# Bias products moved ahead of the sums they open, the selection tree's copies and placements dealt out anew, and the tail ordered by blocks of times

## What is computed

```python
w = weights[subjects]; b = bias[subjects]
h = einsum('bct,bcd->bdt', x, w) + b[:, :, None]
gate = silu((h @ fp8(gate_w)) * gate_scale)      # 256 -> 768
up = (h @ fp8(up_w)) * up_scale                  # 256 -> 768
out = x + ((gate * up) @ fp8(down_w)) * down_scale   # 768 -> 256
```

## Time and profile before

| | us |
|---|---|
| median of 3 runs (lowest, highest) | 52.18 (52.13, 52.43) |
| the profiled execution's own time | 52.42 |
| its span, first to last instruction | 50.6 |
| TensorE (PE) busy | 44.4 (88%) |
| VectorE (DVE) busy | 39.4 (78%) |
| ScalarE (ACT) busy | 25.9 (51%) |
| GpSimd (POOL) busy | 8.5 (17%) |

### The profile page before, as it was taken

One profiled execution on the slowest core, in us unless ns is written; L12 is line 12 of the kernel. 1 busy time (PEld: TensorE's weight loads), 2 busy tenths in 40 slices (PEclk: granted clock), 3 DMA queues, 4 the chain that ended last, 5 costly groups with the idle time before them and its releaser, 6 DMA issues.

```text
span 50.6 us, 667 instructions
## 1 busy us (share of the span) xinstructions
PE 44.4 (88%) x204; PEld 33.2 (66%) x204; DVE 39.4 (78%) x75; ACT 25.9 (51%) x43; POOL 8.5 (17%) x17
## 2 busy tenths in 40 slices
PE   2998999399999999969999999999999999999000
PEld 1331297398878787558878787887878788968000
DVE  2748898996757989999998769999684955896910
ACT  0951408945369095392807809572366394971000
POOL 3039605559600000000000000000000000360000
PEclk9999999999999999999999999999999999999999
DMA  0799999999900000000000000000000000019083
GB/s 0 165 349 366 356 371 402 418 419 414 379 23 0 0 0 0 0 0 13 0 0 0 0 6 0 0 0 0 0 0 0 0 0 0 0 49 371 2 299 115
DMA packets 2579, 5.71 MB, mean 113 GB/s; under 512 B 400, under 2 KB 912, under 8 KB 2576
## 3 DMA queue, kind: packets, MB, share of 16 engines
q1 hardware_dynamic: 2288, 5.53, 29.3%
q10 hardware_dynamic: 288, 0.15, 1.0%
HBM read 4.63 MB, written 1.05 MB: 112 GB/s over the span
## 4 chain that ended last, share of the span: by engine, by line
PE 56%; DVE 22%; DMA 5%; ACT 4%; issue 3%; POOL 3%; DVEq 1%; POOLq 0%
PE gu L538 33%; PE acc L546 19%; DMA subj_i<-in_subjects_dram 5%; DVE fuse L432 4%; PE acc L514 4%; DVE tree_sb L393 3%; POOL cond_bd L323 3%; DVE gu L393 3%; DVE f_lo L440 3%; DVE w_q L355 3%; ACT f_hi L269 2%; DVE res L445 2%; ACT silu L262 1%; DVE cond_bd L400 1%; PE acc L520 1%
## 5 line engine op out<-in xcount | busy, mean ns | idle before, releaser
L538 PE MATMUL gu<-h_hi,w_q 128*128 128x512 f32 (+1 forms) x52 | 15.1, 378 | 0.4 <-DVE w_q L355 0.4
L538 PE MATMUL gu<-h_lo,w_q 128*128 128x512 f32 (+1 forms) x52 | 15.0, 376 | 0.0
L269 ACT CAST f_hi<-fuse 128x512 fp32r<-128x512 f32 (+1 forms) x13 | 7.6, 588 | 12.7 <-DVE fuse L432 12.7
L538 PEld LDWEIGHTS gu<-h_hi,w_q 128*128 128x128 f32 x52 | 9.4, 187 | 2.8 <-issue 0.8
L440 DVE TENSOR_TENSOR f_lo<-fuse,f_hi 128x512 fp32r<-128x512 f32 (+1 forms) x13 | 8.4, 648 | 3.6 <-ACT f_hi L269 3.5
L538 PEld LDWEIGHTS gu<-h_lo,w_q 128*128 128x128 f32 x52 | 9.4, 187 | 2.0
L432 DVE SCALAR_TENSOR_TENSOR fuse<-gu,const_in,silu 128x512 f32<-128x512 f32 (+1 forms) x13 | 9.1, 705 | 1.4 <-issue 0.7
L262 ACT ACTIVATE silu<-gu,const_in 128x512 f32<-128x512 f32 (+1 forms) x13 | 8.4, 646 | 0.9 <-PE gu L538 0.8
L546 PE MATMUL acc<-f_hi,w_q 128*128 128x512 f32 (+1 forms) x26 | 7.9, 380 | 0.0
L546 PE MATMUL acc<-f_lo,w_q 128*128 128x512 f32 (+1 forms) x26 | 7.9, 382 | 0.0
L337 POOL TENSOR_TENSOR res<-y_sc,x_tok 128x512 f32<-128x512 f32 x1 | 1.3, 1297 | 30.4 <-ACT y_sc L283 30.4
(11 more groups left out here) (36 smaller groups left out, 24.6 us busy)
## 6 DMA issues: line engine op xcount, KB each, us to landing
w_in<-in_weights_dram SPq DMA_DIRECT2D x5, 384.0 KB, 6.4
x_sb<-in_x_dram SPq DMA_DIRECT2D x2, 512.0 KB, 4.3
x_tok<-in_x_by_time_dram SPq DMA_DIRECT2D x1, 1024.0 KB, 9.2
out_dram<-res SPq DMA_DIRECT2D x3, 256.0 KB, 2.1
w_in<-in_weights_dram SPq DMA_DIRECT2D x1, 256.0 KB, 3.8
const_in<-in_consts_dram SPq DMA_DIRECT2D x1, 151.0 KB, 2.3
w_in<-in_weights_dram SPq DMA_DIRECT2D x1, 128.0 KB, 5.4
out_dram<-res ACTq DMA_DIRECT2D x1, 128.0 KB, 2.0
```

The costliest lines, as they stand in the source:

```text
L269: nc.scalar.copy(f_hi[:, s % SLOTS, cols], fuse[:, s % SLOTS, cols]).then_inc(f_hi_made, 1)
L538: last = nc.tensor.matmul(gu[:, (s + q) % 2, part, cols], w_q[:, i, col:col + P], h[:, n, k, cols], start=(v == 0 and k == 0), stop=(v == ...
```

## The change

Five parts. (1) The bias products open the sums in `acc` (`bias_of(n)`, two products before `condition(n)`) and the last conditioning product of a bank signals `h_made`; the 12 products on zeros become 9, none tied to the tree; masks move from an `acc` bank to a `gu` bank. (2) ScalarE alone copies the even matrices for both halves, the tree of half 0 is in one bank. (3) Half 1 is placed by ScalarE (j = 0, 1, behind `high_of_h(0, 0)`) and GpSimd (j = 2, 3). (4) On VectorE tile 0 is rounded before `power(1)`; so ScalarE's `big(1)` goes behind `high_of_h(1, 1)`, GpSimd rounds tile 1 in two pieces (gate, up), TensorE waits for each piece apart, `big(4)` and `power(3)` move. (5) In the tail TensorE runs block 0 of step 9 ahead of step 11's gate and up and its block 1 behind; steps 10 and 11 also by blocks; `finish(0, 0)` runs inside step 10 on VectorE, `y_sc` on ScalarE goes behind the last `round_of`; half 1 is finished and stored whole by blocks, in four stores, not five.

```diff
-    WARM = (8, 2, 1, 1)
+    WARM = 9
...
-        tree = [t.rearrange("p (q g d) -> p q g d", g=GH, d=D) for t in (gu_flat[:, 512 + 256:1024 + 256], tree_sb)]
-        bits_ps = acc[:, 3, 0:BITS * G].bitcast(I32).rearrange("p (k g) -> p k g", g=G)
+        tree = [t.rearrange("p (q g d) -> p q g d", g=GH, d=D) for t in (gu_flat[:, 512:1024], tree_sb)]
+        bits_ps = gu[:, 1, 1, 0:BITS * G].bitcast(I32).rearrange("p (k g) -> p k g", g=G)
...
-        POOL_PIECES = ((1, 0, GU),)
+        POOL_PIECES = ((1, 0, GU // 2), (1, GU // 2, GU))
+
+        ACT_BLOCKS = ((0, 1), (0, 1))
+        POOL_BLOCKS = ((), (2, 3))
+        DVE_BLOCKS = ((2, 3), ())
...
             sp.wait_ge(res_dve, 1)
             store(0, 0, TOK)
-            sp.wait_ge(res_pool, 1)
-            store(1, 0, TOK)
             sp.wait_ge(res_dve, 2)
             store(0, TOK, 2 * TOK)
-            sp.wait_ge(res_dve, 4)
-            store(1, TOK + TOK // 2, 2 * TOK)
-            sp.wait_ge(stored, 16 * 5)
+            sp.wait_ge(res_dve, 3)
+            store(1, TOK, 2 * TOK)
+            sp.wait_ge(stored, 16 * 4)
...
             act.wait_ge(const_ld, 16)
-            nc.scalar.copy(tree[0][:, 2:PAIRS], cond_rep[:, 2:PAIRS, 0].unsqueeze(2).to_broadcast([P, 2, GH, D])
-                           ).then_inc(tree_even[0], 1)
-            nc.scalar.copy(tree[1], cond_rep[:, :, 0].unsqueeze(2).to_broadcast([P, PAIRS, GH, D])
-                           ).then_inc(tree_even[1], 1)
+            for n in range(HALVES):
+                nc.scalar.copy(tree[n], cond_rep[:, :, 0].unsqueeze(2).to_broadcast([P, PAIRS, GH, D])
+                               ).then_inc(tree_even[n], 1)
 
...
-                groups = slice(n * GH, (n + 1) * GH)
...
             place(0)
             high_of_h(0, 0)
+            place(1)
             big(0)
             high_of_h(0, 1)
-            big(1)
             high_of_h(1, 0)
             high_of_h(1, 1)
+            big(1)
...
                 silu_of(s)
                 if s == 0:
                     big(2)
+                elif s == 3:
+                    big(4)
                 round_of(s)
-                if s in (1, 2):
-                    big(s + 2)
+                if s == 1:
+                    big(3)
                 elif s in (4, 5):
                     big(s + 1)
 
...
-            act.wait_ge(down_made, HALF_DONE[0] + 1)
-            nc.scalar.activation(y_sc[:], acc[:, 1], ACT.Copy, scale=down_col[:, 1:2]).then_inc(y_scaled, 1)
             for q in range(LAST):
                 silu_of(STEPS - 1, q, PIECES[q])
             for q in range(LAST):
                 round_of(STEPS - 1, q, PIECES[q])
 
-            act.wait_ge(res_dve, 3)
-            act.dma_start(out_rows[:, 1, TOK:TOK + TOK // 2], res[:, 1, 1, 0:TOK // 2]).then_inc(stored, 16)
+
+            act.wait_ge(y0_made, 2)
+            nc.scalar.activation(y_sc[:], acc[:, 1], ACT.Copy, scale=down_col[:, 1:2]).then_inc(y_scaled, 1)
+            act.wait_ge(res_pool, 1)
+            act.dma_start(out_rows[:, 1, 0:TOK], res[:, 1, 0]).then_inc(stored, 16)
...
-            for j in range(J):
-                rows = slice(j * C, (j + 1) * C)
-                nc.gpsimd.tensor_copy(cond_bd[rows, GH:G, j * D:(j + 1) * D], tree[1][rows, 0]
-                                      ).then_inc(cond_placed[1], 1)
+            for j in POOL_BLOCKS[1]:
+                nc.gpsimd.tensor_copy(*block_of(1, j)).then_inc(cond_placed[1], 1)
...
                     if k == 0:
-                        dve.wait_ge(tree_even[n], 2 - n)
+                        dve.wait_ge(tree_even[n], 1)
...
             dve.wait_ge(const_ld, 16)
-            nc.vector.tensor_copy(tree[0][:, 0:2], cond_rep[:, 0:2, 0].unsqueeze(2).to_broadcast([P, 2, GH, D])
-                                  ).then_inc(tree_even[0], 1)
             dve.wait_ge(bits_made, 2)
             select(0)
             dve.wait_ge(bd_zeroed, 1)
-            place(0)
+            dve.wait_ge(tree_level[0], BITS)
+            for j in DVE_BLOCKS[0]:
+                nc.vector.tensor_copy(*block_of(0, j)).then_inc(cond_placed[0], 1)
             select(1)
...
             power(0, 0, GU)
             rest_of_h(0, 0)
-            power(1)
             add_big(0)
             take_big(0)
+            power(1)
             rest_of_h(0, 1)
             rest_of_h(1, 0)
             rest_of_h(1, 1)
...
                     take_big(2)
+                    power(3)
...
+                elif s == STEPS - 2:
+                    dve.wait_ge(x_tok_ld, 16)
+                    dve.wait_ge(y0_made, 1)
+                    finish(0, 0)
                 rest_of(s)
...
                     take_big(1)
                 elif s == 1:
-                    power(3)
                     add_big(2)
...
-            dve.wait_ge(x_tok_ld, 16)
-            dve.wait_ge(down_made, HALF_DONE[0] + 1)
-            finish(0, 0)
...
-            dve.wait_ge(y_made, 1)
-            finish(1, 0)
-            dve.wait_ge(y_made, 2)
-            for cols in PIECES:
-                finish(1, 1, cols)
+            for b in range(TB):
+                dve.wait_ge(y1_made, b + 1)
+                finish(1, b)
...
-            pe.wait_ge(warm_set, 1)
-            keep_warm(WARM[0])
-            for k in range(BITS):
-                pe.wait_ge(tree_level[0], k + 1)
-                keep_warm(WARM[k + 1])
...
-            for n in range(HALVES):
+            def bias_of(n):
+
+                pe.wait_ge(ones_made, 1)
+                pe.wait_ge(bias_placed, n + 1)
+                for k in range(KC):
+                    nc.tensor.matmul(acc[:, KC * n + k], ones_r[:], bias_tok[:, n * TOK // D:(n + 1) * TOK // D],
+                                     start=True, stop=False, skip_group_check=True)
+
+            def condition(n):
                 pe.wait_ge(cond_placed[n], J)
...
-                    bank = acc[:, KC * n + k]
                     for g in range(GH):
-                        nc.tensor.matmul(bank[:, g * P:(g + 1) * P], x_sb[:, n * GH + g, k * P:(k + 1) * P],
-                                         cond_bd[:, n * GH + g], start=(g == 0), stop=False,
-                                         skip_group_check=True)
-                    if k == 0:
-                        pe.wait_ge(ones_made, 1)
-                        pe.wait_ge(bias_placed, n + 1)
-                    nc.tensor.matmul(bank, ones_r[:], bias_tok[:, n * TOK // D:(n + 1) * TOK // D],
-                                     start=False, stop=True, skip_group_check=True).then_inc(h_made, 1)
+                        last = nc.tensor.matmul(acc[:, KC * n + k, g * P:(g + 1) * P],
+                                                x_sb[:, n * GH + g, k * P:(k + 1) * P], cond_bd[:, n * GH + g],
+                                                start=False, stop=(g == GH - 1), skip_group_check=True)
+                    last.then_inc(h_made, 1)
+
+            pe.wait_ge(warm_set, 1)
+            keep_warm(WARM)
+            for n in range(HALVES):
+                bias_of(n)
+                condition(n)
...
-                wait_quant(pe, i, 0)
                 for v, part in GU_ORDER[s < 2]:
+                    if v == 0:
+                        wait_quant(pe, i, part * KC * P)
...
+            def down_times(s, b):
+
+                pe.wait_ge(f_lo_made, s + 1)
+                down_block(s, 0, b)
+                return down_block(s, 1, b)
...
-            down(STEPS - 1 - LAG)
+
+
+            s = STEPS - 1
+            for i in (IC - 2, IC - 1):
+                wait_quant(pe, i, GU)
+            down_times(s - 2, 0).then_inc(y0_made, 1)
             for q in range(LAST):
-                gate_up(STEPS - 1, q, PIECES[q])
-            down(STEPS - 2)
-
-            s = STEPS - 1
-            wait_quant(pe, STEP[s][0], GU)
-            for q in range(LAST - 1):
-                for v, part_made in enumerate((f_hi_made, f_lo_made)):
-                    pe.wait_ge(part_made, s + q + 1)
-                    for b in range(TB):
-                        down_block(s, v, b, PIECES[q])
-            pe.wait_ge(f_hi_made, STEPS + LAST - 1)
-            down_block(s, 0, 0, PIECES[LAST - 1])
-            pe.wait_ge(f_lo_made, STEPS + LAST - 1)
-            down_block(s, 1, 0, PIECES[LAST - 1]).then_inc(y_made, 1)
-            down_block(s, 0, 1, PIECES[LAST - 1])
-            down_block(s, 1, 1, PIECES[LAST - 1]).then_inc(y_made, 1)
+                gate_up(s, q, PIECES[q])
+            down_times(s - 2, 1).then_inc(y0_made, 1)
+            down_times(s - 1, 0)
+            pe.wait_ge(f_hi_made, s + 1)
+            down_block(s, 0, 0, PIECES[0])
+            pe.wait_ge(f_lo_made, s + 1)
+            down_block(s, 1, 0, PIECES[0])
+            pe.wait_ge(f_hi_made, s + 2)
+            down_block(s, 0, 0, PIECES[1])
+            down_times(s - 1, 1)
+            pe.wait_ge(f_lo_made, s + 2)
+            down_block(s, 1, 0, PIECES[1]).then_inc(y1_made, 1)
+            for v in range(2):
```

(35 more changed lines are left out.)

7 lines of the change are left out of this document (5 added, 2 removed).

## The result

| | before | after |
|---|---|---|
| median of 20 runs (lowest, highest), us | 52.46 (52.13, 52.62) | 52.05 (51.92, 52.48) |
| profiled execution, us | 52.42 | 51.97 |
| its span, us | 50.6 | 50.2 |

The ratio of after to before is 0.9953, 95% interval 0.9933 to 0.9973: half a per cent faster, where 3.4% was forecast. 1.8 us were expected and 0.4 came. The profile after shows an opening that went almost to the hundredth as worked out, and two places behind it where the gain is given back.

What follows compares the result with a forecast made beforehand. TensorE was taken to bound the kernel from 22.00 us on, with gains only ahead of that and in the tail. Last finish 1.56 to 2.06 sooner, less 0.1 for the store, taken as 1.8: 52.18 to 50.4 us, range 49.9 to 51.4.

Steps and rivals of the forecast that it cites:

- Tree of half 0: Opening: ScalarE's copy of all pairs lets VectorE's first masked copy start at 3.72, not 4.04; 0.32 us won.
- Bias first: Conditioning of half 0: bias products leave the end of each bank, so rounding of h starts at 7.19, 0.55 sooner.
- Half 1 on two engines: Placement of half 1 by ScalarE and GpSimd: condition(1) starts at 8.72, not 9.73; 1.01 us won.
- Tile 0 first: VectorE's rounding before the gate: tile 0 ready at 10.58, first gate product at 10.64 against 12.09; 1.45 us won.
- Tile 1 late: GpSimd rounds tile 1 from 12.47 to 15.5 or 15.7; step 2's up part waits 0.2 to 0.4 us.
- TensorE's speed: Rival on both halves' conditioning: TensorE stays at its lower speed, time 53.6 us; chance 0.05.
- Tile 2 for step 4: VectorE's rounded weights come at 20.20, so step 4 starts at 20.3 instead of 22.00; 1.7 us won.
- Tail: Last products, finishes and stores: last finish ends at 46.15 or 46.65 against 48.21; larger last store costs 0.1 us.
- ends some 0.5 before: In the tail, the path over ScalarE and GpSimd (y_sc, add, store) ends some 0.5 us before the last store.
- the wait of the first tail product for f_lo: In the tail, step 9's pair of block 0 waits for the rest of f; 0.2 or 0.7 us lost.
- The gap put down to "issue" on VectorE: Steps 4 to 10: a 0.73 us gap ahead of a fuse; if it stays, VectorE's line is only about 1.1 ahead.
- VectorE's line sets the end: Rival: slips at tile 2 or take_big(3), the gap and tail losses leave 1.0 to 1.2 won, 51.1 us; chance 0.18.

Runs made afterwards that it cites:

- run 9: Changed kernel with 2 products on zeros instead of 9; ratio to the kernel before 1.0195 from two of four executions, median of all four 53.71 us.
- Run 4: Changed kernel with GpSimd only copying tile 1's gate and up columns, their fp8 rounding left out; ratio to the kernel before 0.9883.
- run 5: Changed kernel with VectorE's power(1) ahead of add_big(0) and ScalarE's big(1) behind high_of_h(0, 1) again, so GpSimd rounds tile 1 earlier; ratio to before 0.9874.
- run 10: Changed kernel with half 1 placed by GpSimd alone again (four copies); ratio to the kernel before 1.0143.
- run 1: Changed kernel with all tail edits (part 5) undone; ratio to before 0.9899 without its two longest executions, median of all twelve 51.91 us.
- run 2: Kernel before with only the changed tail (part 5); ratio to the kernel before 1.0098.
- run 3: Changed kernel without ScalarE's 256 KB store of block 1 of half 0, output incomplete; ratio to the kernel before 0.9805.

## Why the prediction was wrong, point by point

The direction was right, and so were the steps up to 15.3 us:

- *Tree of half 0*: 3.72 forecast, 3.81 measured; the copy into PSUM took 0.59, the signal more than the 0.06 I had taken. Half 0's products at 6.07 instead of 6.00.
- *Bias first*: h rounded from 7.26 (forecast 7.19), bias products hidden at 5.08 and 7.88. Right.
- *Half 1 on two engines*: 8.47 (forecast 8.72, its lower bound 8.4). Right.
- *Tile 0 first*: ready at 10.56, first gate product at 10.61 (10.58 and 10.64). Right.
- *Tile 1 late*: GpSimd from 12.15 to 15.29 (12.47 to 15.5 or 15.7); the up part of step 2 starts at 15.38 without a loss. Slightly better than forecast.
- *TensorE's speed*: no loss; but run 9 shows that it was not a remote case.

**The step that failed first is "Tile 2 for step 4".** I moved VectorE's line by 1.41 with every instruction at its old duration and came to 20.20. Two of them became 0.48 and 0.53 longer, and the weights came at 20.84. TensorE waited 0.73, and step 4 came at 20.99 instead of 20.3: 0.7 of the 1.7 forecast was gone. Run 4 gives 0.44 of it back; that its own first gate product is 0.16 late hides some more, and the rest is not accounted for. The wrong assumption stood a part earlier: I had moved GpSimd's work by 1.5 us and asked only when it would be ready, not what it would lie beside. Before, it ran from 10.64 to 13.45, beside h_lo, which reads one operand from PSUM; those took their usual 0.69. In the changed kernel its additions and subtractions from 13.8 on read both operands from SBUF. I had the rule in hand, in the part on half 1, and used half of it: the Trainium skill ("GPSIMD Engine Reference", Key points) names, beside two-port instructions, those "with two SBUF inputs". Runs 4 and 5 agree with that half in both directions: longer beside GpSimd (0.90, 1.22), not longer without it (0.42, 0.69).

How much longer can be read from the rows, and it is no fixed factor. The instruction that starts second ends later, by about the time that it overlaps with the first, less some 0.15; the first keeps its length. In the changed kernel the addition at 13.79 overlaps GpSimd's of 13.67 to 14.41 by 0.62 and is 0.48 longer; f_lo at 14.61 overlaps the one of 14.49 to 15.29 by 0.68 and is 0.53 longer. In run 10 f_lo at 14.81 overlaps GpSimd's addition until 15.18 by 0.37 and is 0.22 longer; the subtraction at 15.64 overlaps until 16.30 by 0.66 and is 0.53 longer. It goes the other way too: run 10's GpSimd instruction at 15.25 overlaps that f_lo by 0.47 and is 0.31 longer, and in the kernel before GpSimd's addition at 10.64 began 0.30 before VectorE's subtraction was over the earlier trace rows: it took 1.44 where its subtraction of the same size took 1.29, and VectorE kept its 0.69. GpSimd's ends are rough in a profile, but these cases agree within a few hundredths.

**The second is the store term of "Tail".** I took 0.1 for a last store of 256 KB instead of 128, and it was 0.75. Not the size counted but the traffic: of the 1 MB output 768 KB are issued within 0.66 us. I had written that the path over ScalarE and GpSimd "ends some 0.5 before", and taken that for harmless. It ended 0.47 before (46.58 for 47.05), just as forecast, and a store that is issued 0.47 before the last one is exactly what the last one waits behind: at 375 GB/s its 256 KB are 0.7 us. Runs 1 to 3 show it from three sides.

The remaining terms were mis-sized less. The last finishes begin at 45.64, forecast 44.7 or 45.2: the 0.7 from step 4, and the wait of the first tail product for f_lo (0.3, at 40.97; forecast 0.2 to 0.7). Two whole finishes took 1.41 (1.42). The gap put down to "issue" on VectorE was 0.3 instead of 0.73 and cost nothing.

The sum as measured in the profiled pair: 1.48 won at the first gate product, 0.47 lost up to step 4, 0.15 won from there to the last finish (1.16), 0.75 lost in the stores: 0.41 of span.

Of the rivals, "VectorE's line sets the end" was the nearest: it named that line and the place (tile 2), with a slip of 0.3 where 0.6 came, but not its cause; and no rival held the stores. What stays open: what parts the two groups of executions of the kernel before, what lies around the span of the kernel in run 1, and how run 10's loss divides.

## What to carry to other kernels

When work is moved in time on GpSimd, list what VectorE does in the new window: beside GpSimd's instructions, VectorE's with both operands in SBUF waited for nearly the whole overlap when they started second (up to 0.53 us each here), those with one in PSUM did not. Look at the order of the starts as well as at the overlap. When a tail is reordered, add up the bytes that are issued in the last two microseconds, not only the time of the last store; a store that "ends a little before" the last is the one to move far forward or to keep small. And a tail can lose more by a store (0.75 here) than it wins on the engines (0.15).
